# Reordering the statistics and the fp16 splits of the first chunks in a fused attention and FFN layer

## The reference

```
xn  = layernorm(x)                       # x: 4 x 1024 x 256, float32, no gain
q   = rotary(xn @ Wq) / 4                # 16 heads of 16
kv  = rotary(xn @ Wkv)                   # serves as keys and as values
att = softmax(q kv^T) kv                 # per batch and head, 1024 tokens
y   = x + (att @ Wout + bout) + ffn(xn)
ffn(xn) = (silu(xn @ Wg^T) * (xn @ Wu^T)) @ Wd^T    # hidden 768, int32 weights / 127
```

## Time and profile before

| | before |
|---|---|
| median of 3 runs | 831.03 us (830.79 to 833.65) |
| the profiled execution | 833.87 us |
| its span in the trace | 832.0 us |
| TensorE busy over the span | 798.9 us (96%) |
| VectorE, ScalarE, GpSimd busy | 736.4, 691.5, 267.5 us (89%, 83%, 32%) |
| granted TensorE clock, mean | 0.994 of full speed |

### The profile page before, as it was taken

The page is one execution under the profiler, slowest core; times in us unless marked ns, Lnnn a source line. Parts: engine busy times, 40 slices in busy tenths (PEclk is TensorE's granted clock), DMA queues, the critical chain, the costliest instruction groups (busy, mean ns, idle before and its releaser), DMA issues.

```text
span 832.0 us, 19132 instructions
## 1 busy us (share of the span) xinstructions
PE 798.9 (96%) x7316; PEld 296.3 (36%) x7316; DVE 736.4 (89%) x891; ACT 691.5 (83%) x1270; POOL 267.5 (32%) x504
## 2 busy tenths in 40 slices
PE   4988999999999999999999999999999999999997
PEld 2344555445333333333333333333333333333234
DVE  5877888888899999999999999999999999999702
ACT  4655555545799999999999999999999999999982
POOL 3785778887120001101222222222222222222210
PEclk9998999999999999999999999999999999999999
DMA  9456455554111111111221122221222212221222
GB/s 312 120 117 147 108 124 128 127 127 104 33 32 37 29 37 30 31 30 45 56 58 50 49 53 58 54 51 49 55 54 58 53 49 51 56 58 50 81 74 75
DMA packets 111680, 60.55 MB, mean 73 GB/s; under 512 B 71372, under 2 KB 101900, under 8 KB 111588
## 3 DMA queue, kind: packets, MB, share of 16 engines
q1 hardware_dynamic: 111588, 59.32, 28.2%
HBM read 28.57 MB, written 16.90 MB: 55 GB/s over the span
## 4 chain that ended last, share of the span: by engine, by line
PE 91%; ACT 3%; POOL 2%; DMA 1%; DVE 1%; issue 1%; SPq 0%; DVEq 0%; ACTq 0%; POOLq 0%
PE ps L759 34%; PE ps L776 19%; PE ps L741 15%; PE ps L636 9%; PE ps L650 4%; ACT arena L1021 2%; PE ps L613 1%; PE ps L614 1%; PE ps L615 1%; PE ps L609 1%; POOL arena L1340 1%; PE ps L685 1%; DMA x_all<-x_dram 1%; PE ps L787 1%; PE ps L803 1%
## 5 line engine op out<-in xcount | busy, mean ns | idle before, releaser
L1176 DVE TENSOR_REDUCE negmax<-ps 128x2 f32<-128x1024 f32 x512 | 588.8, 1212 | 6.5 <-PE ps L776 6.4
L1021 ACT ACTIVATE arena<-ps 128x512 f32<-128x512 f32 x1024 | 555.4, 595 | 31.7 <-PE ps L741 9.9
L759 PE MATMUL ps<-arena 128*32 128x256 f32 x4072 | 326.5, 392 | 2.4 <-issue 2.2
L741 PE MATMUL ps<-qs,ks 51*128 51x512 f16 x1024 | 197.9, 382 | 3.3 <-ACT arena L1021 2.1
L776 PE MATMUL ps<-ks,qs 48*128 48x512 f16 x972 | 189.4, 386 | 0.0
L759 PEld LDWEIGHTS ps<-arena 128*32 128x32 f32 x4072 | 80.6, 108 | 127.9 <-issue 126.8
L776 PEld LDWEIGHTS ps<-ks,qs 48*128 48x128 f16 x972 | 46.6, 92 | 195.0 <-DVE negmax L1176 140.1
L636 PE MATMUL ps<-arena,side 128*128 128x512 f16 x384 | 89.7, 382 | 4.3 <-DVE side L1121 4.3
L1444 POOL TENSOR_TENSOR arena<-arena,x_all 128x256 f32<-128x256 f32 x22 | 16.0, 728 | 232.0 <-ACT arena L1042 232.0
L741 PEld LDWEIGHTS ps<-qs,ks 51*128 51x128 f16 x1024 | 50.7, 93 | 77.8 <-ACT arena L1021 45.9
L1374 POOL TENSOR_TENSOR mparts<-rowmax,munit 128x16 f16<-128x16 f32 x32 | 7.1, 222 | 210.4 <-DVE rowmax L1186 210.4
(11 more groups left out here) (117 smaller groups left out, 516.7 us busy)
## 6 DMA issues: line engine op xcount, KB each, us to landing
parts_d<-arena SPq DMA_DIRECT2D x64, 128.0 KB
x_all<-x_dram SPq DMA_DIRECT2D x8, 512.0 KB, 9.0
qs<-parts_d SPq DMA_DIRECT2D x64, 64.0 KB, 1.9
ks<-parts_d SPq DMA_DIRECT2D x64, 64.0 KB, 1.9
o_d<-arena SPq DMA_DIRECT2D x124, 32.0 KB
arena<-o_d SPq DMA_DIRECT2D x24, 128.0 KB
arena<-inv_d SPq DMA_DIRECT2D x48, 64.0 KB
out_dram<-arena SPq DMA_DIRECT2D x24, 128.0 KB, 1.8
```

The lines of the kernel that those rows point to most:

```text
L741: mm = pe.matmul(ps[:, score_bank(place(p, kt, 2 * half + a)), :], ks[ring][top:top + ROWS, kt * P:(kt + 1) * P], qs[ring][top:top + ROWS, ...
L759: mm = pe.matmul(ps[32 * j:32 * j + 32, 7, cols], vstage[pl % 2][:, j % 2, kt, :], probs[PER_STEP * (kt % PBUF) + j][:, cols], start=(kt = ...
L1021: act.activation(probs[PER_STEP * (kt % PBUF) + j], ps[:, score_bank(place(p, kt, j)), :], ACT.Exp).then_inc(exp_done, 1)
L1176: dve.tensor_reduce(negmax[pl % 2][:, h, :, kt], ps[:, bank:bank + 2, :], AX.X, ALU.max, negate=True).then_inc(max_done, 1)
```

## The change

Four edits, all in the first phase:

- `ROOTS`: the first group is tiles 8 to 11 (chunk 2 alone), the second tiles 12 to 31. `normalise(3)` thus waits for the second group. VectorE takes the four moments of chunk 2 between the gated products of chunk 0 (three behind `gated(0, 1)`, one behind `gated(0, 2)`) where it took eight at the end of chunk 0; of the other twenty it takes three behind `rope_chunk(1)`, ten in pairs ahead of `gated(1, 1)` to `gated(1, 5)` and seven at the end of chunk 1. `add_ffn(0, t)` moves from behind `gated(1, 1)` to ahead of `gated(1, 0)`, as in the later chunks.
- GpSimd does `low_x(c+1)` ahead of `low_qk(c, t)` from chunk 1 on.
- SyncE does `turn_x(c+1)` ahead of `turn_qk(c)` in every chunk.
- The four low parts of chunk 0's q and kv: tiles 0 and 1 on GpSimd behind `low_hid(0, 1)` and `low_hid(0, 2)`, tiles 2 and 3 on VectorE (`low_first_qk`) behind `gated(0, 2)` and at the end of the chunk.

```
-ROOTS = ((2 * CT, 4 * CT), (4 * CT, 8 * CT))
+ROOTS = ((2 * CT, 3 * CT), (3 * CT, 8 * CT))
...
-                if c:
-                    turn_qk(c)
                 if c + 1 < NCHUNK:
                     turn_x(c + 1)
-                if c == 0:
-                    turn_qk(0)
+                turn_qk(c)
...
-                act.wait_ge(shift_done, 1 if c == 0 else 2 if c == 1 else 3 if c < 4 else 4)
+                act.wait_ge(shift_done, 1 if c == 0 else 2 if c == 1 else 3 if c < 3 else 4)
...
+            def low_first_qk(t):
+
+                dve.wait_ge(wud_ready, 1)
+                dve.wait_ge(qk_hi_done, t + 1)
+                dve.tensor_tensor(qk_lo[:, :, t, :], qk[:, t, :].rearrange("p (g n) -> p g n", g=4), qk_hi[:, :, t, :],
+                                  ALU.subtract).then_inc(qk_lo_done, 1)
...
                 rope_chunk(c)
-                if c > 1:
+                if c == 1:
+                    moments(3 * CT, 3)
+                if c:
                     for t in range(CT):
                         add_ffn(c - 1, t)
                 gated(c, 0)
                 units = lead_units(c)
                 for j in range(1, KH):
+                    if c == 1:
+                        moments(3 * CT + 1 + 2 * j, 2)
...
                     gated(c, j)
-                    if c == 1 and j == 1:
-                        for t in range(CT):
-                            add_ffn(0, t)
-                    elif c == 1:
-                        moments(4 * CT + 3 * (j - 2), 3)
-                    if c == 0 and j in (3, 4):
+                    if c == 0 and j == 1:
+                        moments(2 * CT, 3)
+                    elif c == 0 and j == 2:
+                        moments(3 * CT - 1, 1)
+                        low_first_qk(2)
+                    elif c == 0 and j in (3, 4):
                         low_w(j - 3)
                 if c == 0:
-                    moments(2 * CT, 2 * CT)
+                    low_first_qk(3)
                 elif c == 1:
-                    moments(7 * CT, CT)
+                    moments(6 * CT + 1, 2 * CT - 1)
...
+                if c + 1 < NCHUNK and c:
+                    low_x(c + 1)
                 if c:
                     for t in range(CT):
                         low_qk(c, t)
                 keep_values(c)
-                if c + 1 < NCHUNK:
-                    low_x(c + 1)
+                if c == 0:
+                    low_x(1)
                 for j in range(KH):
                     low_hid(c, j)
-                if c == 0:
-                    for t in range(CT):
-                        low_qk(0, t)
+                    if c == 0 and j in (1, 2):
+                        low_qk(0, j - 1)
```

## The result

The changed kernel takes 825.99 us at the median of 5 runs (825.44 to 826.87); the kernel before took 831.6 us beside it (830.79 to 833.65). The ratio is 0.9924, with a 95% interval from 0.9910 to 0.9938: faster by 0.6 to 0.9%. The forecast was 821.8, with a range of 819.8 to 825.2, so the time lies 0.8 us above the range. The sign and the place were right, the size was not. The profiled execution of the changed kernel took 825.99 us, its span is 824.1.

The account below looks back on a forecast made before the run. TensorE was taken as the bound, dense from 80 us on, with 11.1 us winnable before; less 0.3 (chunk 0) and 1.4 (chunk 2) this gave 9.4, 9.2 with thin covers: 821.8 us on the 831.03 median, range 819.8 to 825.2.

Parts of the forecast that it names:

- gaps of 1.40, 2.38 and 5.23 us: TensorE's delays in chunk 1 ahead of block 2, block 5 and `project(2)`, in that order; all were to close.
- 2.06 of clock: Chunk 2's projection took 7.24 us, not 5.18, at the lower clock after idle stretches; the 2.06 us were to go.
- GpSimd's cover: Chunk 0: `low_hid(0, 5)` moves from 39.0 to 40.2 us, hidden because `down(0)` starts only at 42.2.
- the term of the rotary embedding: Chunk 1, VectorE: starts at 38.5 us instead of 40.30, takes 8.8 to 8.9, ends at 47.3.
- the first gap: Chunk 1, the 1.40 us ahead of block 2: closes with 0.3 us to spare.
- rival 2: VectorE and GpSimd block each other at `low_first_qk`: `project(1)` 1.2 us later, gain 7.7, time 823.3 us; chance 0.15.
- GpSimd's term: Chunk 1: `low_x(2)` takes 2.27 us, `low_hid(1, 0)` starts at 53.3 to 53.8, block 5's gap closes with 0.4 spare.
- right chain: Chunk 2: late statistics and GpSimd work delay the third `lead` to 79.2 us, wanted at 77.8; 1.4 us given back.
- Sum: Whole kernel: 11.1 - 0.3 - 1.4 = 9.4 us gained, 9.2 with half a step of the thin covers.
- Rival 1: The cover in chunk 2 holds, so nothing is given back there: gain 10.8 us, time 820.2; chance 0.13.
- Rival 3: GpSimd stays the bound in chunk 1, `low_hid(1, 0)` at 57.45: 825.1 us, 827.2 if the clock falls; chance 0.13.
- Rival 4: Chunks 2 to 6: `low_x` blocks VectorE's rotary stretch; 833.2 us if all of it lands on TensorE; chance 0.04.

Follow-up runs that it names:

- b0_before: The kernel before, run again with no edit: 832.09 us, ratio 0.9998.
- a2_short_x2: The changed kernel with the low part of chunk 2's x cut to one column of 128 per tile, so not fully computed: 824.32 us, one run.
- a3_gp_order: The changed kernel with GpSimd's old order, q and kv ahead of x, SyncE keeping the new one: 826.37 us, ratio 0.9933 to the kernel before.
- a4_spread: The changed kernel with the statistics in three groups of roots and the moments spread further: 826.59 us, ratio 0.9923 to the kernel before.
- a1_values: The changed kernel with the copy of the values moved behind `low_hid(c, 2)` on GpSimd: 824.51 us, ratio 0.9903 to the kernel before.
- a0_after: The changed kernel, run again with no edit: 826.23 us, ratio 0.9922 to the kernel before.
- e2_order: The kernel before with only the order changed, x ahead of q and kv on SyncE and GpSimd: 830.12 us, ratio 0.9977.
- e4_no_stats: The changed kernel without its statistics part, so order and low parts together: 829.25 us, ratio 0.9964 to the kernel before.
- e3_lows: The kernel before with only the change to chunk 0's low parts: 829.35 us, ratio 0.9963.

## Why the prediction was wrong

Counted from the origin (28.49 in the trace the forecast used), point by point:

- **Place, and what is won there: right.** The gaps of 1.40, 2.38 and 5.23 us and the 2.06 of clock were real in every execution of before (b0_before), and the last three went.
- **Chunk 0: right for TensorE.** `down(0)` starts at 13.46 from the origin, 13.44 before; I had 13.7. `low_first_qk` took 0.75 and 0.93 us (forecast 0.64). But GpSimd's cover was thinner than I said: two of its instructions took 1.60 us each beside VectorE, not 1.13 to 1.24. `gated(0, 5)` waits 1.15 us for `low_hid(0, 2)`, which my count didn't have, and `down(0)` waits 0.53 for `low_hid(0, 5)`, which I had called hidden with 2 us to spare. `project(1)`, 0.7 us earlier than before, pays for it. The low turn went out at 37.93, which looks like the forecast 38.0 but is 10.10 from the origin against 9.5, 0.6 late; that cost nothing, as x had 5 us to spare.
- **Chunk 1: the term of the rotary embedding was mis-sized.** I took its length from before, 8.8 us, and so 0 for the first gap. It starts when I said (37.82, or 9.99 from the origin; forecast 10.0) but ends 1.1 us late, at 47.77: 2.24 us for the two last adds, which took 1.28, and 1.35 for the first, which took 1.14. The edit itself brought GpSimd's `low_x(2)` over the two last. My ground, that GpSimd's reading did not lengthen most such adds, was a misreading of the rows: GpSimd was idle from 46.68 (43.45 + 3.23) to 49.26, so the two adds at 48.64 lay for the most part beside an idle engine, and the one at 43.59, beside a busy one, took 1.14. I had written the mutual blocking down as rival 2, but priced it only on the new instruction, not on the ones that the moved `low_x` would meet. `project(2)` came at 30.29 from the origin instead of 29.3: 1.0 us. a2_short_x2 and a3_gp_order show the cause of the long adds. GpSimd's term was too small by as much: `low_x(2)` took 3.17 us and not 2.27, and `low_hid(1, 0)` starts at 26.4 from the origin, where I had 24.8 to 25.3, a cover that I had called 0.4 us thin. VectorE's wait hides this in the changed kernel; a4_spread, where it is gone, shows it as 1.08 us at block 5.
- **Chunk 2: right chain, one step mis-sized.** I named the chain `inverse(3)`, x(3), q and kv, values, `low_hid(2, 0)`, reduction, third `lead`, and gave it 1.4 us. The waits were 1.20 ahead of block 2 and 1.31 at the lead, 2.5 together (2.7 by the starts). That block 2's falls inside the loss was right, since the chain alone sets the third lead; the chain was longer. `low_hid(2, 0)` starts at 77.70, 49.87 from the origin instead of 47.7, 2.2 us late: 1.0 inherited from chunk 1, 0.3 in VectorE and ScalarE, 0.9 because `low_x(3)` waited for and lay beside the adds (from x split at 69.02 to 72.26, 3.24 us instead of 2.27). The lead came 2.3 us later than forecast (53.03 and 50.7), 1.0 of it TensorE's own lateness from chunk 1, so 1.3 was lost here. a1_values shows that the chain is GpSimd's.
- **Sum.** The sum was 9.4; less 1.0 in chunk 1 and 1.3 in chunk 2 it is the 7.1 of the traces (67.81 to 60.70, and 67.81 to 60.71 in b0_before and a0_after). At the medians it is 5.6 us beside the first runs of before, 6.7 in a0_after, and 6.3 if 825.99 is set against the wide base of 832.33, which comes from other runs. The interval, 5.2 to 7.5, holds all of them. The origin itself lies between 27.03 and 28.95 us in the eleven traces whose edits come behind it, which is more than these differences; how much of the 0.8 us between 7.1 and 6.3 it explains, runs without a trace can't tell.
- **The base.** 831.03 was the median of three runs; over 26 it is 832.33. That hid 1.3 us: on the wider base the forecast would have been 823.1, and 7.1 would give 825.2. So of the 4.2 us between 821.8 and 825.99, 2.1 are the two mis-sized terms (9.2 less 7.1), 1.3 the base, and 0.8 stay open.
- **Rivals.** Rival 1 (cover in chunk 2 holds) fell. Rival 2 was the right mechanism at other instructions; its own sign, a late `project(1)`, did not come (7.59 from the origin, 8.26 before). Rival 3 fell (`low_hid(1, 0)` at 54.27, not 57.45). Rival 4 fell for the chunks behind the second: 20.00 of 20 from 100 us to 180, and the same 67.48 us from `down(2)` to `down(7)` as before.
- **The page of the Trainium skill** ("SBUF — State Buffer", "Who interferes with whom") says that a VectorE operation with two SBUF inputs and a GpSimd operation reading SBUF contend for one read interface. The traces agree for the adds: 1.28 us for two when GpSimd's piece is short (a2_short_x2) or elsewhere (a3_gp_order), 2.24 when it is long and beside them, and `low_x` 0.5 us late at its start there (69.50 for an input ready at 69.02).

**Why the parts don't add.** Alone: statistics 0, order 2.2, low parts 3.0; the last two together 2.9; all three 6.7 (832.89 to 826.23 in a0_after). Order and low parts each bring x(2) about 5 us earlier, and either suffices. What then ends last is VectorE, 2 to 2.7 us late in chunks 1 and 2, and the moments are its load.

## What to carry to other kernels

When a long wait goes, list every engine's lateness at the next points where TensorE meets it: an edit that brings nothing alone can be the next bound's. A step moved to another time must be priced with the instructions it will lie beside, theirs as well as its own: here a moved subtraction cost two adds nearly 1 us and itself 0.5 to 0.9. And take the base from more than three runs when the forecast's range is a few microseconds.

## What the runs showed of the hardware

Two things were new to me. The granted clock can fall behind a wait of 2.1 us in otherwise dense matmuls (e2_order, e4_no_stats: 32 matmuls in 8.75 us instead of 7.07, a loss of 1.7), while it stayed at 1.00 over the waits of 1.0 to 1.3 us in the changed kernel (its windows above); so a wait that grows from 1.2 to 2.1 us can cost three times its growth. It need not: behind 2.65 us in e2_order, 2.21 and 2.00 in e3_lows and 2.38 in a3_gp_order the next 8 matmuls took 1.89 or 1.90 us, which is full clock. What decides between the two, no run here shows. And GpSimd and VectorE slow each other in both directions: the same GpSimd subtraction of 128x512 takes 1.13 us alone and 1.6 beside VectorE's chunk 0, two rotary adds 1.28 and 2.24 us.
